# A scan kernel on one core: the chunk tables are read after the weight steps, and two groups of scan inputs begin two and three half slots sooner

## The chip, the cores and the metric

The kernel runs on one core of one Trainium2 chip. The metric is the device time of one execution in microseconds (us). TensorE is called PE, VectorE DVE, ScalarE ACT, GpSimd POOL, and SyncE, which here issues the transfers, SP.

## What is computed

Two transformer blocks run over `x` of shape (2, 1024, 512). The first half of block 0 is a gated delta-rule scan over 1024 positions for each of two batches, with 64 state columns; everything that the change touches belongs to it.

```python
k = _l2norm(x @ Wk.T); v = x @ Wv.T; q = _l2norm(x @ Wq.T)
alpha = exp(8 * sigmoid(x @ Wa_w.T + Wa_b) * log(sigmoid(lam) + 1e-8))
def step(H, inp):                      # one position
    pred = einsum('bk,bkv->bv', q_t, H)
    surprise = sigmoid(sum((v_t - pred) ** 2))
    delta = k_t[:, :, None] * (v_t - einsum('bk,bkv->bv', k_t, H))[:, None, :]
    H = a * H + (1.0 - a) * (surprise * delta)
    return H, einsum('bk,bkv->bv', q_t, H)
...
wq_gu = ternary_quant(w_gate_up); wq_p = ternary_quant(w_proj)   # the weights of the feed-forward part of block 0
```

After the scan come that block's feed-forward part with ternary weights, then block 1 (an attention part with a running sum, and a feed-forward part).

## The kernel before

`head()` does three things at once: it prepares the inputs of the scan, it runs the first half of the scan, and it turns the first layer's weights into ternary ones. `groups()`, which is not touched, does the second half of the scan and all the rest.

**Scan.** A batch's 1024 positions are eight chunks of 128. `head()` does chunks 0 to 3 (`HC = 4`) of both batches. A chunk is solved by five rounds (`R = 5`). In a round each batch b goes through one chain: PE multiplies (`residual`, L659, two matmuls written as four passes), DVE subtracts (`residual`, L929 in the first round, L932 in the others), ACT squares and takes a tanh (`surprise`, L470 and L472), DVE weighs (`weighted`, L943), and PE may multiply again. Behind the fifth round of a chunk a new state is made (PE `states` L668, DVE L954, then PE L659 on the new state), and in the first round of the next chunk PE also makes two outputs (`outputs`, L677 and L678).

**Half slots.** The order of each engine's queue is written out by hand by the number h of a half slot. Half slot h = 2 * (n * R + r) + b belongs to round r of chunk n of batch b, so that 40 half slots, 0 to 39, make up the scan, ten for a chunk. Half slots from -28 to -1 come before it. On DVE the order in a pair is: `residual` of batch 0, inputs(h), late(h), `residual` of batch 1, `weighted` of batch 0, inputs(h + 1), late(h + 1), `weighted` of batch 1. On PE it is `residual`, means(h), inputs(h), sections(h), and behind these `states` and `outputs` where there are any.

**Inputs of the scan.** Four groups u = 0 to 3 of 512 positions are prepared in stages i, and `BEGIN` says in which half slot a group reaches stage 10:

```python
    BEGIN = (-26, -18, 6, 16)
...
    def stages(h):
        return [(u, h - BEGIN[u] + 10) for u in range(NG)]
```

Groups 0 and 1 feed the four chunks of this scan; groups 2 and 3 feed the chunks that `groups()` does later. The stages are: 0 to 4 statistics (DVE L721 to L729), 6 to 9 normalization (DVE L737), 10 to 13 feature-major turns (PE L552, ACT L378), 14 to 17 projections (PE L568, four matmuls each), 18 to 25 DVE and ACT work on them with the cumulated sum in 20 (PE L582, L586), and then for each of the group's four chunks a transposition (PE L596 to L599 in stages 25, 27, 29, 31, copied out by ACT L418 and L419) and a product (PE L605 in stages 26, 28, 30, 32). DVE reads the product's bank `in_t1`, multiplies by a mask and writes the chunk's table `LT`:

```python
        def masked(u, j):
            dve.wait_ge(l_full, u * NJ + j + 1)
            ...
            nc.vector.tensor_tensor(at_chunk(scan, "LT", ORDER[u] * NJ + j), pl[:, 0:3 * P].rearrange("p (k t) -> p k t", t=P),
                                    mask[:], ALU.mult).then_inc(l_out, 1)
```

The next product into that bank waits for `l_out`, and so do some turns of the features that use the same bank.

**Weights.** 112 ternary steps (`ternary`, L829 to L842, one DVE instruction of 128x512 or 128x1024 each) are dealt out evenly over half slots -18 to 39 by `late(h)`, mostly two to a half slot; `means(h)` is their matmul L614 on PE. `late(h)` also finishes one section of the modulation in half slot 7 (L104, which signals `mod_out`); the first projection of group 2 waits for that signal.

Of the kernel before, what the change touches and what calls it, by code (L numbers as in the profile page):

```python
# [124 lines left out]
def head(nc, dram, keep, scan, sems, whole, ctx):  # L125
# [96 lines left out]


    HALVES = 2 * HC * R
    BEGIN = (-26, -18, 6, 16)
    FROM, TERNARY_FROM, SECTIONS_FROM = -28, -18, -7
    STEPS = WSTEPS * PAIRS

    def stages(h):

        return [(u, h - BEGIN[u] + 10) for u in range(NG)]

# [5 lines left out]
    def ternary_step(n):  # L238

        if n == 0:  # L240
            return 0, 0
        q, i = divmod(n - 1, WSTEPS)
        if q == PAIRS - 1:
            return q, i + 1
        return (q + 1, 0) if i == 3 else (q, i + 1 if i < 3 else i)
# [3 lines left out]
    def late_section(h):  # L249

        n, stage = divmod(h - SECTIONS_FROM, KD + 1)
        return (n + 2, stage) if 0 <= n < EARLY_SECTIONS - 2 else (None, None)
# [106 lines left out]
    def _(act):  # L359
# [73 lines left out]
        def log_decays():  # L433
            act.wait_ge(lam_sig, 3)
            nc.scalar.activation(lam[:], lam[:], ACT.Ln).then_inc(act_steps, 1)
            act.wait_ge(consts, 6)
            nc.scalar.activation(junk[0][:, 0, 0:1], ones[:, 0:1], ACT.Exp)
# [48 lines left out]
        for h in range(FROM, 0):  # L486
            if h == BEGIN[0] + KD:
                log_decays()
# [226 lines left out]
    def _(dve):  # L715
        c = Count(dve, dve_steps)

        def norm_stats(u, j):
            if j == 0:
                dve.wait_ge(x_in[u % 2], 16 * (u // 2) + 16)  # L720
            c.did(nc.vector.bn_stats(stats[:, j], x[:, u % 2, j]))  # L721
# [28 lines left out]
        def values(u):  # L750
            dve.wait_ge(proj, u + 1)
            nc.vector.tensor_copy(chunk(scan["v"], u), pp[:, :, 2 * NS:3 * NS]).then_inc(v_out, 1)
# [68 lines left out]
        def ternary(q, i):  # L821


            if (q, i) != (0, 0):
                dve.wait_ge(w_steps, number[q, i] - 1)
            wt, scale = keep["wt"][:, 2 * q:2 * q + 2], wscale[:, q % 2]
            if i < 2:
                dve.wait_ge(mean_full, 2 * q + i + 1)
                ins = nc.vector.tensor_scalar(scale[:, i], pm[0], 1e-8, None, ALU.max, ALU.max,  # L829
                                              accum_out=wsmax[:, 2 * q + i:2 * q + i + 1])  # L830
            elif i == 2:
                ins = nc.vector.tensor_tensor(whash[:], scale, wabs[:, q % 2], ALU.is_lt)
            elif i == 3:
                dve.wait_ge(w_cast, 3 * q + 2)
                ins = nc.vector.tensor_tensor(whash[:], whash[:], wsgn[:, q % 2], ALU.mult)
            elif i == 4:
                ins = nc.vector.tensor_tensor(whash[:], whash[:], scale, ALU.mult)
            elif i == 5:
                dve.wait_ge(w_cast, 3 * q + 3)
                ins = nc.vector.tensor_tensor(whash[:], whash[:], wt, ALU.subtract)  # L840
            else:
                ins = nc.vector.tensor_tensor(wt, wt, whash[:], ALU.add)  # L842
            ins.then_inc(w_steps, 1)
# [46 lines left out]
        def inputs(h):  # L890
            for u, i in stages(h):
                if u and 0 <= i < NJ:
                    norm_stats(u, i)
                elif u and i == 4:
                    norm_sums(u)
                elif u and 6 <= i < 6 + NJ:
                    norm_rows(u, i - 6)
                elif i == 18:
                    gate_in(u)
                    values(u)  # L900
                elif i == 19:
                    lengths(u)
                    log_alphas(u)
                elif i == 20:
                    keys(u, 0)
                    keys(u, 1)
                elif i == 21:
                    before(u)
                    betas(u, 0)
                elif i == 22:  # L910
                    betas(u, 1)
                    if u:
                        growths(u).then_inc(ready, 1)
                    else:
                        c.did(growths(u))
                elif i in (23, 24):
                    tilted(u, 2 * (i - 23))
                    tilted(u, 2 * (i - 23) + 1)
                elif i == 25:
                    spans(u, 0)  # L920
                    spans(u, 1)
                elif i in (26, 28, 30, 32):
                    masked(u, (i - 26) // 2)

        def residual(n, r, b):
# [37 lines left out]
        def late(h):  # L963
            for i in share(h, STEPS):
                ternary(*ternary_step(i))
            if late_section(h)[1] == KD:
                section(late_section(h)[0])

        for h in range(FROM, 0):
            if h == BEGIN[0] + 8:  # L970
                log_decays()
            inputs(h)
            late(h)
        for n in range(HC):
            for r in range(R):
                h = 2 * (n * R + r)
# [1492 lines left out]
def build(nc, dram):  # L2469
    with ExitStack() as whole:  # L2470
# [46 lines left out]
        with ExitStack() as ctx:  # L2517
            head(nc, dram, keep, scan, sems, whole, ctx)
# [58 lines left out]
```

## Time and profile before

| what | us |
|---|---|
| median of 3 runs | 1183.12 (1183.0 to 1185.53) |
| the profiled execution | 1185.58 |
| its span, first to last instruction | 1184.0 |
| up to the scan's first DVE instruction (L929 at 77.30) | 77.3 |
| the 40 half slots of the scan, 77.30 to 200.07 | 122.8 |
| everything behind it | 983.9 |

PE is busy for 1077.5 us of the span, DVE for 869.1, ACT for 525.2 and POOL for 171.3. These are averages over stages that differ: the scan in `head()` is a chain that passes between PE, ACT and DVE for two batches in turn, with the other work laid in between. What an edit is worth there is read from which wait ends last in a half slot.

### The profile page before, as it was taken

The numbers are of one execution on the slowest core, as the hardware profiler recorded it, in microseconds if no ns is written. First come the engines' busy times: TensorE is split into PE (matmuls) and PEld (weight loads), VectorE is DVE, ScalarE is ACT, GpSimd is POOL, SyncE is SP. The second block draws the span as 40 slices with busy tenths as digits, with TensorE's granted clock in tenths as the row PEclk, the third lists the DMA queues.
The fourth block names the chain that finished last, engine by engine and source line by source line (L and its number), as shares of the span: only waits on it lengthen the run. The fifth ranks groups of instructions, "written<-read, shape, count | busy, mean of one in ns | idle before, by whom it ended". The sixth has DMA issues, their size and how long they took to land. (4 is left out here: it accounts for less than half of the span.)

```text
span 1184.0 us, 12999 instructions
## 1 busy us (share of the span) xinstructions
PE 1077.5 (91%) x4360; PEld 522.0 (44%) x4360; DVE 869.1 (73%) x1602; ACT 525.2 (44%) x1103; POOL 171.3 (14%) x143
## 2 busy tenths in 40 slices
PE   6788778799979999888998999999998999999997
PEld 2435545444534444334443454444444444444443
DVE  3887776756756778797687899577887677785654
ACT  3655654445525385244263364164444263531421
POOL 3100000211202221030121131122102000100100
PEclk9888765699998999899998999999999999999999
DMA  8511111532400333222130003012010011010000
GB/s 272 180 54 36 54 36 27 187 107 72 126 0 19 118 92 104 69 79 89 56 95 18 27 27 98 16 40 101 27 63 10 1 60 30 18 72 0 1 36 35
DMA packets 47618, 75.53 MB, mean 64 GB/s; under 512 B 8416, under 2 KB 16096, under 8 KB 47424
## 3 DMA queue, kind: packets, MB, share of 16 engines
q1 hardware_dynamic: 47264, 74.62, 19.9%
q0 software_dynamic: 288, 0.09, 0.2%
q8 instruction: 35, 0.57, 0.2%
q14 instruction: 31, 0.25, 0.1%
HBM read 66.16 MB, written 8.54 MB: 63 GB/s over the span
## 5 line engine op out<-in xcount | busy, mean ns | idle before, releaser
L1517 PE MATMUL g_g<-h,wt 128*128 128x512 f16 x1728 | 401.2, 381 | 5.8 <-DVE hid L1824 3.1
L1517 PEld LDWEIGHTS g_g<-h,wt 128*128 128x128 bf16 (+1 forms) x1728 | 168.4, 98 | 223.8 <-issue 35.5
L1531 PE MATMUL g_d<-wt,parts 128*128 128x512 bf16 (+1 forms) x864 | 208.5, 384 | 4.5 <-DVE tmp L1654 2.7
L2144 ACT ACTIVATE parts<-hid 128x512 f16<-128x512 f32 x108 | 68.0, 629 | 303.3 <-DVE hid L1824 303.2
L1439 PE MATMUL g_o<-shared 128*128 128x512 f32 x384 | 183.3, 621 | 14.4 <-DVE tmp L1613 6.4
L1817 DVE SCALAR_TENSOR_TENSOR hid<-th,g_g 128x512 f32<-128x512 f32 x108 | 73.6, 681 | 135.8 <-ACT th L2137 135.7
L1531 PEld LDWEIGHTS g_d<-wt,parts 128*128 128x128 f16 x864 | 84.1, 99 | 114.5 <-issue 16.6
L2258 POOL TENSOR_TENSOR acc<-acc,sqh 128x512 f32<-128x512 f32 x52 | 79.6, 1532 | 297.1 <-ACT sqh L2150 297.1
L1439 PEld LDWEIGHTS g_o<-shared 128*128 128x128 f32 x384 | 75.0, 199 | 98.4 <-issue 72.5
L1829 DVE TENSOR_TENSOR parts<-hid,parts 128x512 f16<-128x512 f32 x108 | 89.6, 830 | 26.0 <-ACT parts L2144 25.9
L2238 POOL TENSOR_TENSOR g_rstd<-g_var,g_power 128x4 f32<-128x4 f32 x20 | 24.2, 1210 | 328.9 <-DVE g_var L1557 328.9
L1824 DVE SCALAR_TENSOR_TENSOR hid<-hid,fac,g_g 128x512 f32<-128x512 f32 x64 | 46.9, 732 | 23.6 <-PE g_g L1517 22.7
L2137 ACT ACTIVATE th<-g_g 128x512 f32<-128x512 f32 x64 | 37.6, 588 | 51.7 <-PE g_g L1517 51.5
L1448 PE MATMUL g_o<-shared 128*128 128x512 f32 x128 | 57.8, 594 | 2.7 <-DVE shared L1901 2.7
L2137 ACT ACTIVATE th<-g_g,sgate 128x512 f32<-128x512 f32 x44 | 30.1, 684 | 62.2 <-PE g_g L1517 62.2
L1892 DVE RECIPROCAL shared<-shared 128x256 f32<-128x256 f32 x32 | 55.8, 1743 | 0.0
L2246 POOL TENSOR_TENSOR h<-hf,h 128x512 f16<-128x512 f32 x32 | 41.2, 1293 | 85.1 <-ACT hf L2037 79.2
L2157 ACT ACTIVATE shared<-g_o 128x512 f32<-128x512 f32 x32 | 19.0, 593 | 62.4 <-PE g_o L1439 62.3
L1824 DVE SCALAR_TENSOR_TENSOR hid<-hid,sgu,g_g 128x512 f32<-128x512 f32 x44 | 32.0, 728 | 16.4 <-PE g_g L1517 16.0
L1569 DVE TENSOR_TENSOR x<-x,tmp 128x512 f32<-128x512 f32 x60 | 39.9, 688 | 1.0
L2150 ACT ACTIVATE sqh<-hid 128x512 f32<-128x512 f32 x64 | 39.3, 614 | 0.4 <-PE g_o L1428 0.3
L1847 DVE SCALAR_TENSOR_TENSOR shared<-shared,mix 128x512 f32<-128x512 f32 x48 | 36.8, 809 | 2.4 <-ACT shared L2065 2.3
(329 smaller groups left out, 1511.5 us busy)
## 6 DMA issues: line engine op xcount, KB each, us to landing
shared<-in_w SPq DMA_DIRECT2D x48, 256.0 KB, 2.7
x<-in_codes SPq DMA_DIRECT2D x32, 264.0 KB, 3.1
w_raw<-in_wt SPq DMA_DIRECT2D x16, 512.0 KB, 3.5
x<-in_wmod SPq DMA_DIRECT2D x7, 1024.0 KB, 5.2
wmod<-in_wmod SPq DMA_DIRECT2D x5, 1024.0 KB, 11.5
codes_f<-x SPq DMA_DIRECT2D x32, 132.0 KB, 1.7
gates<-in_x SPq DMA_DIRECT2D x4, 1024.0 KB, 8.2
shared<-in_wt SPq DMA_DIRECT2D x8, 512.0 KB, 4.7
```

The costliest lines, as they stand in the source:

```text
L1439: mm = nc.tensor.matmul(dst[:], w1[:, n % 4, k], xmix[:, w, k], start=(k == 0), stop=(k == KD - 1))
L1448: mm = nc.tensor.matmul(dst[:], rw[:, k, j * P:(j + 1) * P], wo[:, k, :], start=(k == 0), stop=(k == KD - 1))
L1517: mm = nc.tensor.matmul(pg[i][:], wide[:, k, o:o + P], h16[f % 2][:, s, k], start=(s == 0 and k == 0), stop=(s == 1 and k == KD - 1))
L1531: mm = nc.tensor.matmul(pd[j][:], parts16[:, t % 3, s, j * P:(j + 1) * P], wd[:, m, :], start=(m == 0 and s == 0), stop=(done and s == 1))
L1817: nc.vector.scalar_tensor_tensor(hid[:, t % 2], th[:], 1.0, pg[0][:], ALU.add, ALU.mult).then_inc(gate_free, 1)
L1824: nc.vector.scalar_tensor_tensor(hid[:, t % 2], hid[:, t % 2], const, pg[1][:], ALU.mult, ALU.mult).then_inc(up_free, 1)
L1829: nc.vector.tensor_tensor(parts16[:, t % 3, 1], hid[:, t % 2], parts16[:, t % 3, 0], ALU.subtract).then_inc(lo_ready, 1)
L1892: c.did(nc.vector.reciprocal(part, part))
L2137: nc.scalar.activation(th[:], pg[0][:], ACT.Tanh, scale=scale).then_inc(th_ready, 1)
L2144: nc.scalar.activation(parts16[:, t % 3, 0], hid[:, t % 2], ACT.Copy).then_inc(hi_ready, 1)
L2246: nc.gpsimd.tensor_tensor(h16[f % 2][:, 1, k], hf[:, k % 2], h16[f % 2][:, 0, k], ALU.subtract).then_inc(hl_ready, 1)
L2258: nc.gpsimd.tensor_tensor(acc[:], acc[:], sqh[:, m % 2], ALU.add).then_inc(acc_ready, 1)
```

## The change

The read of the product's bank is taken out of the stages and put in a function of its own, `tables(h)`, which DVE runs behind the ternary steps of the half slot. `BEGIN` of group 2 goes from 6 to 4, and that of group 3 from 16 to 13, on all engines. No instruction is added or removed; PE's, ACT's, DVE's and POOL's work is the same, in another order.

```diff
-    BEGIN = (-26, -18, 6, 16)
+    BEGIN = (-26, -18, 4, 13)
     FROM, TERNARY_FROM, SECTIONS_FROM = -28, -18, -7
@@
                 elif i == 25:
                     spans(u, 0)
                     spans(u, 1)
-                elif i in (26, 28, 30, 32):
+
+        def tables(h):
+            for u, i in stages(h):
+                if i in (26, 28, 30, 32):
                     masked(u, (i - 26) // 2)
@@
         def late(h):
             for i in share(h, STEPS):
                 ternary(*ternary_step(i))
+            tables(h)
             if late_section(h)[1] == KD:
                 section(late_section(h)[0])
```

Four lines are added ahead of them, so L929, L932, L943, L954 and L961 of before are L932, L935, L946, L957 and L964 in the changed kernel.

The first place is DVE's queue in the last chunk of the scan, half slots 34 to 36. In the kernel before:

```order
L932 TENSOR_TENSOR shared<-shared,sc 128x128
L812 TENSOR_TENSOR shared<-in_t,mask 128x384
L832 TENSOR_TENSOR whash<-wscale,wabs 128x1024
L835 TENSOR_TENSOR whash<-whash,wsgn 128x1024
L932 TENSOR_TENSOR shared<-shared,sc 128x128
L943 SCALAR_TENSOR_TENSOR shared<-shared,sur 128x64
L829 TENSOR_SCALAR wscale,wsmax<-mean_ps 128x512
L837 TENSOR_TENSOR whash<-whash,wscale 128x1024
L943 SCALAR_TENSOR_TENSOR shared<-shared,sur 128x64
L932 TENSOR_TENSOR shared<-shared,sc 128x128
L812 TENSOR_TENSOR shared<-in_t,mask 128x384
L840 TENSOR_TENSOR whash<-whash,wt 128x1024
```

The same half slots, 34 to 36, in the changed kernel:

```order
L935 TENSOR_TENSOR shared<-shared,sc 128x128
L832 TENSOR_TENSOR whash<-wscale,wabs 128x1024
L835 TENSOR_TENSOR whash<-whash,wsgn 128x1024
L935 TENSOR_TENSOR shared<-shared,sc 128x128
L946 SCALAR_TENSOR_TENSOR shared<-shared,sur 128x64
L829 TENSOR_SCALAR wscale,wsmax<-mean_ps 128x512
L837 TENSOR_TENSOR whash<-whash,wscale 128x1024
L812 TENSOR_TENSOR shared<-in_t,mask 128x384
L946 SCALAR_TENSOR_TENSOR shared<-shared,sur 128x64
L935 TENSOR_TENSOR shared<-shared,sc 128x128
L840 TENSOR_TENSOR whash<-whash,wt 128x1024
L842 TENSOR_TENSOR wt<-wt,whash 128x1024
```

Group 3's table reads (L812) stood directly behind `residual` of batch 0 in half slots 32, 34, 36 and 38. They now stand behind the ternary steps in half slots 29, 31, 33 and 35, ahead of `weighted` of batch 1, and half slots 36 to 39 have none.

The second place is PE's queue at the end of the second chunk and the start of the third (half slots 18 to 20; `residual` is L659, a projection L568 x4, a feature turn L552 x4, a chunk's transposition L596 to L599, its product L605). Before:

```order
L659 MATMUL sc<-shared,LT 128x64 x2
L552 MATMUL in_t<-ident,gates 128x128 x4
L659 MATMUL sc<-shared,LT 128x64 x2
L614 MATMUL mean_ps<-wabs,groupmean 128x512
L552 MATMUL in_t<-ident,gates 128x128 x4
L668 MATMUL sc<-shared 64x64
L659 MATMUL sc<-shared 128x64 x2
L614 MATMUL mean_ps<-wabs,groupmean 128x512
L568 MATMUL in_proj<-w,ln_hT 128x256 x4
L668 MATMUL sc<-shared 64x64
```

In the changed kernel:

```order
L614 MATMUL mean_ps<-wabs,groupmean 128x512
L596 MATMUL in_t<-ident,kq_sq 64x128
L597 MATMUL in_t<-ident,kq_sq 64x128
L598 MATMUL in_t<-ident,qy_tilde 64x128
L599 MATMUL in_t<-ident,b_tilde 64x128
L568 MATMUL in_proj<-w,ln_hT 128x256 x4
L668 MATMUL sc<-shared 64x64
L659 MATMUL sc<-shared 128x64 x2
L614 MATMUL mean_ps<-wabs,groupmean 128x512
L605 MATMUL in_t<-shared,bT 128x384
L568 MATMUL in_proj<-w,ln_hT 128x256 x4
L668 MATMUL sc<-shared 64x64
```

Group 3's projections have moved from half slots 20 to 23 to half slots 17 to 20, and group 2's first transposition and first product, from 21 and 22, now stand in 19 and 20 ahead of the two matmuls L668 that make the new states.

The third place is DVE's queue ahead of the scan, where group 0's third table read and group 1's stage 22 stand (half slot -6). Before:

```order
L829 TENSOR_SCALAR wscale,wsmax<-mean_ps 128x512
L812 TENSOR_TENSOR LT<-in_t,mask 128x384
L785 TENSOR_TENSOR wt<-wt 128x256
L880 TENSOR_TENSOR g<-eh 64x3
L885 TENSOR_SCALAR gh<-g 64x3
L832 TENSOR_TENSOR whash<-wscale,wabs 128x1024
L835 TENSOR_TENSOR whash<-whash,wsgn 128x1024
L793 TENSOR_TENSOR wt<-shared,wt 128x4x64 x2
```

In the changed kernel:

```order
L829 TENSOR_SCALAR wscale,wsmax<-mean_ps 128x512
L785 TENSOR_TENSOR wt<-wt 128x256
L880 TENSOR_TENSOR g<-eh 64x3
L885 TENSOR_SCALAR gh<-g 64x3
L721 BN_STATS ln_stats<-gates 128x6
L832 TENSOR_TENSOR whash<-wscale,wabs 128x1024
L835 TENSOR_TENSOR whash<-whash,wsgn 128x1024
L812 TENSOR_TENSOR LT<-in_t,mask 128x384
L793 TENSOR_TENSOR wt<-shared,wt 128x4x64 x2
```

The table read has moved behind six instructions of its half slot, one of which (L721, group 2's first statistics) comes from half slot -4.

## Rows read from the trace of the kernel before

**Rows 1.** Windows by stage: length, busy time and count by engine, PE clock, DMA.

```profile
77.30:105.38 28.08, 22.48 (x99) 11.67 (x97) 24.39 (x72) 18.17 (x50) 1.39 (x1) 0.83 0.12 39
105.38:136.16 30.78, 24.08 (x116) 19.46 (x117) 24.11 (x74) 19.30 (x61) 3.23 (x2) 0.78 0.14 52
136.16:171.34 35.18, 28.56 (x124) 20.16 (x123) 25.41 (x71) 19.13 (x66) 1.85 (x1) 0.74 0.16 46
171.34:200.07 28.73, 25.46 (x80) 16.40 (x79) 20.77 (x54) 14.34 (x56) 0.00 (x0) 0.50 0.08 19
```

**Rows 2.** DVE's waits in the scan (77.3 to 200.07): total us, times, longest.

```profile
DVE shared L932 <- PE sc L659: 8.0, 7, 2.5
DVE shared L812 <- PE in_t L605: 7.2, 8, 1.3
DVE shared L929 <- PE sc L659: 5.8, 6, 1.2
DVE shared L954 <- PE sc L668: 3.7, 2, 1.9
DVE LT L812 <- PE in_t L605: 1.6, 3, 1.1
```

**Rows 3.** Timeline of DVE, 190 to 195.3 us: start, duration, what, [idle before].

```profile
190.15 0.28 DVE L932 TENSOR_TENSOR shared<-shared,sc 128x128 f32<-128x128 f32 x1
...
191.49 0.56 DVE L812 TENSOR_TENSOR shared<-in_t,mask 128x384 f32<-128x384 f32 x1 [1.06 <-PE in_t L605]
...
193.29 0.28 DVE L932 TENSOR_TENSOR shared<-shared,sc 128x128 f32<-128x128 f32 x1
...
195.22 0.28 DVE L932 TENSOR_TENSOR shared<-shared,sc 128x128 f32<-128x128 f32 x1
```

**Rows 4.** Timeline of PE over the same round, 188.7 to 193.9 us.

```profile
188.76 1.11 PE L659 MATMUL sc<-shared,LT 128*128 128x64 f32 x4
189.81 1.65 PE L605 MATMUL in_t<-shared,wt 64*128 64x384 f32 x2
191.38 1.11 PE L659 MATMUL sc<-shared,LT 128*128 128x64 f32 x4
192.29 0.63 PE L614 MATMUL mean_ps<-wabs,groupmean 128*128 128x512 bf16 x1
192.71 0.42 PE L596 MATMUL in_t<-ident,wt 128*64 128x128 f32 x1
...
193.35 0.42 PE L599 MATMUL in_t<-ident,wt 128*64 128x128 f32 x1
...
193.82 1.11 PE L659 MATMUL sc<-shared,LT 128*128 128x64 f32 x4
```

**Rows 5.** Timeline of PE and DVE: projections, a product, and a new state at a chunk's start.

```profile
105.27 3.78 PE L568 MATMUL in_proj<-w,ln_hT 128*128 128x256 f32 x8
...
136.46 3.62 PE L568 MATMUL in_proj<-w,ln_hT 128*128 128x256 f32 x8
...
140.41 0.28 DVE L954 SCALAR_TENSOR_TENSOR shared<-sc,gh,shared 64x64 f32<-64x64 f32 x1 [1.82 <-PE sc L668]
...
145.69 0.91 PE L605 MATMUL in_t<-shared,bT 64*128 64x384 f32 x2
...
149.19 1.89 PE L568 MATMUL in_proj<-w,ln_hT 128*128 128x256 f32 x8
```

**Rows 6.** Timeline at half slots 7 to 9: the last early section and what follows.

```profile
98.82 0.16 DVE L104 TENSOR_SCALAR modv<-in_proj 128x8 f32<-128x8 f32 x1
99.44 1.12 PE L659 MATMUL sc<-shared,LT 128*128 128x64 f32 x4 [1.08 <-DVE shared L943]
101.42 0.28 DVE L932 TENSOR_TENSOR shared<-shared,sc 128x128 f32<-128x128 f32 x1
```

**Rows 7.** Timeline of DVE ahead of the scan: the longest table wait there.

```profile
62.78 0.56 DVE L812 TENSOR_TENSOR LT<-in_t,mask 128x384 f32<-128x384 f32 x1 [1.55 <-PE in_t L605]
```

**Rows 8.** Window of the long stretch in which PE's granted clock is 0.50.

```profile
157.20:222.00 64.80, 52.42 (x164) 33.82 (x163) 46.52 (x132) 28.74 (x104) 3.16 (x4) 0.50 0.33 105
```

## The prediction

> **What bounds the kernel now.** I read the windows by stage first. The change touches only `head()`: the 77.3 us ahead of the scan, and the scan's four chunks of 28.08, 30.78, 35.18 and 28.73 us, 122.8 in all [rows 1]. What comes later has the same queues, so it should move as a block with the end of the scan. In the scan no engine is full: DVE is busy for 24.39, 24.11, 25.41 and 20.77 us of the four chunks, 94.7 of 122.8. The list of DVE's waits says where the other 28 are: 8.8 us in 11 waits for a table's product (7.2 + 1.6), 13.8 for the residual matmuls (8.0 + 5.8) and 3.7 for the new states [rows 2]. Only the 8.8 is what the moved table read waits for.
>
> Next I read the last chunk, where the pattern is clean. Batch 0's residual is subtracted at 190.15, DVE waits 1.06 us for the product, reads it at 191.49, does two ternary steps and takes batch 1's residual at 193.29; the other half slot, without a table, lasts from 193.29 to 195.22 [rows 3]. A round is 5.06 us. PE in such a round: residual of batch 0 from 188.76, product from 189.81, residual of batch 1 from 191.38, mean from 192.29, transposition from 192.71, next residual at 193.82 [rows 4]. The last of the transposition's four passes, which follow each other by 0.21, starts at 193.35, so PE could have gone on at 193.56. It is full for 4.80 of 5.06 us. So the visible DVE wait of 1.06 is worth only 0.26 per round as long as the round holds a product and a transposition.
>
> **The parts of the change, each costed.**
>
> *Ahead of the scan: -1.0 us.* The longest table wait there is 1.55 us [rows 7]. Behind it DVE has work that needs nothing of the product: two ternary steps, 1.3 us together (193.29 less 191.49 and the 0.5 that a read keeps DVE [rows 3]), and group 1's stage 22. Taken in front they cover all of it, at most -1.55. Against it, group 2's sums (some 0.5 us of small DVE instructions) are now done before half slot 0. If PE or ACT is late next, nothing is left: 0 is the other bound.
>
> *First chunk, 28.08 us: +1.5.* Group 2's first two projections come to half slots 8 and 9. The first waits for the section signal at 98.82, while PE would start batch 1's residual at 99.44 and DVE take it at 101.42 [rows 6]. A row L568 x8 is one projection, four matmuls in two passes each: 3.6 us of PE at the lower clock, 1.8 at the upper (3.62 and 1.89 [rows 5], whose last pass overlaps what follows by 0.1). At the lower clock PE is at the residual at 98.9 + 3.6 = 102.5 and DVE gets it at about 103.3, 1.9 us late; at the upper clock it is there at 101.4 and costs nothing. To this come 0.65 us more of DVE's stage work in this chunk, and some 0.6 us of table waits go. Bounds 0 and +3; I take +1.5, since the residual at 99.44 takes 1.12 us [rows 6], the lower clock's time (1.11 at 188.76 [rows 4], where the clock is 0.50 [rows 8]).
>
> *Second chunk, 30.78 us: +0.5.* Group 3's first three projections come to half slots 17 to 19 and leave 21 to 23. These half slots were 2.2 to 2.5 us long, filled by DVE; a projection of 1.8 beside a residual of 0.5 fits, one of 3.6 does not and costs 2.4. In both runs of four projections the first one is long (105.27 and 136.46); the other six are short like the last (149.19 [rows 5]). With one long one, half slot 17 costs +2.4. Half slot 10 then has group 2's third projection in place of its first and saves 1.8. Bounds -1.5 and +5 (all three long); I take +0.5.
>
> *Third chunk, 35.18 us: -4.5.* Here PE holds 9.8 us of DVE's time (35.18 less 25.41). Three projections leave half slots 21 to 23, where DVE waited for residuals behind them, and the table waits are covered by 1.3 us of ternary steps. What has to stay is the latency of the states, about 1 us for each first residual (L929: 5.8 in 6 times [rows 2]). New is that in half slot 20 a product stands with the last projection ahead of L668, for which DVE already waits 1.82 us [rows 5]. At the upper clock mean, projection and product are 0.2 + 1.8 + 0.9 behind the residual, and the state is ready some 3.1 us after it instead of 4.25 (136.16 to 140.41). So DVE's busy time of 25.4, 0.5 more of stage work, and about 3.5 of waits: 29.4, a gain of 5.8. At the lower clock half slot 20 is 1.8 us worse than now, the cumulated sum in 23 is 1 us longer, and the gain is 2. I take 4.5, nearer to the first, because the run of projections has begun three half slots earlier.
>
> *Last chunk, 28.73 us: -3.5.* The four rounds from 180.1 on last 20.2 us. Two of them keep a product and a transposition and stay PE's: 4.80 each. The other two, half slots 36 to 39, are bare: 1.93 us (193.29 to 195.22) and 1.5 (3.13 of the half slot from 195.22, less a wait of 1.05 and the read's 0.5), 3.45 a round. That makes 16.5, a gain of 3.7. In half slots 30 and 31, a product of 1.57 takes the place of a transposition of 0.85 ahead of the outputs, with DVE idle behind it: +0.7, less what DVE's two moved instructions of stage 24 (0.67) free in half slot 30. Bounds -2.8 and -4.2. The read in an odd half slot stands ahead of batch 1's `weighted`; by PE's order (residual, mean, product: 0.9 + 0.4 + 1.6) it is ready 2.0 us after that residual is taken, when two ternary steps and `weighted` (1.8) are nearly through. It costs nothing there while PE is full.
>
> **Sum:** -1.0 + 1.5 + 0.5 - 4.5 - 3.5 = -7.0 us. The profiled execution took 1185.58 around a span of 1184.0 and would take 1178.6. It lies 2.5 above the median of the runs, 1183.12, which gives 1176.1. SP's and POOL's queues keep their order: no transfer is moved past another. POOL's two roots per group come as much sooner as their inputs.
>
> **The clock.** From 157.2 to 222.0 the granted clock is 0.50, the 1.2 GHz level, although PE is busy for 52.4 of these 64.8 us [rows 8] and full for 4.80 of 5.06 in a round [rows 4]. The Trainium skill says otherwise: its page TensorE: Matmul & The Clock Gate (Part 1: The HAM clock gate) has sustained activity release the throttle and idleness bring it back, and by it the rounds from 180 on would be at 2.4 GHz. The trace does not agree there; by that rule the two full rounds would shrink from 4.80 to DVE's own 3.9 each (3.45 and a read of 0.5), 1.8 us more gained. By the same rule the emptier half slots 12 to 16 of the changed kernel would send the projections behind them to the lower level, which speaks against the change. The sum above rests on the rows, and the two directions are the last two rivals.
>
> **The rivals.**
>
> *A, the forecast* (-3 to -11, about 1176): a chance of 0.60.
>
> *B, the waits only change their name* (0.16). PE holds the rounds, the table waits come back as waits for residuals, and group 3's work in the middle costs what it frees at the end. For it: 4.80 of 5.06 [rows 4]. Against it: the two bare rounds and the three projections that leave the crowded third chunk. It gives 4 x 0.26 = 1 for the waits and about 1 for the rest, -2: 1181.
>
> *C, slower: the projections run at the lower clock* (0.10). Half slots 12 to 16 keep only small PE work and the clock falls ahead of half slot 17. Each further long projection costs 1.8 us on PE. Today two of eight are long; with six of eight that is 7.2, which is the whole gain, and half slot 20 at the lower level adds 1.8 plus 0.8 for the product: +3, 1186. The point from which it decides is four further long ones. For it: with two levels, means of 0.83, 0.78 and 0.74 say that PE is at the lower one for a third to a half of the first three chunks, and for all of the last (0.50 [rows 1]). Against it: each run so far has risen after its first.
>
> *D, more* (0.14): the clock stays at the upper level into the last chunk or nearly all projections find it. The last chunk's full rounds shrink by 1.8 and the others reach their bounds: -12, 1171.
>
> **The numbers.** The likeliest is 1176.1. The low end adds the good bounds, -1.5 + 0 - 1.5 - 5.8 - 4.2 = -13, 1170; the high end the bad ones short of all at once, -0.5 + 3 + 2 - 2 - 2.5 = 0, stretched by 1 for C: 1184. A's own range is 1172 to 1180. A measurement of this kernel tells 0.2% (2.4 us) from no change, that is, below 1180.8 is faster. Of A nearly all, all of D and a third of B are faster: 0.78. The rest of B and the mild end of C are the same: 0.13. Slower: 0.09.
>
> **What would show it.** The scan's first subtraction should come at 76.3 and the second chunk's start later than 105.38 - 1.0 by 1 to 2 us. From the 20th half slot to the 30th it should take some 31 us, and from the 30th to the end 25, with the last two rounds near 3.5 each. Table reads should have almost no wait of their own in the half slots with two ternary steps, except in half slots 20 and 29 to 35. Of the eight projections two or three should have rows of 3.6. The prediction is wrong if the clock's pattern in half slots 8 to 23 puts more than four projections at the lower level, if the waits for L668 in half slots 19 and 20 grow by more than a microsecond each, or if what follows the scan does not move with it.

## The result and the profile after

| what | before | after |
|---|---|---|
| median of 4 runs each, us | 1184.32 (1183.0 to 1186.87) | 1170.39 (1164.84 to 1171.01) |
| ratio, 95% interval | | 0.9878 (0.9857 to 0.9898) |
| the profiled execution and its span | 1185.58, 1184.0 | 1170.35, 1168.8 |

The changed kernel is 13.9 us faster. The forecast was 7.0, so the time, 1170.4, lies at the low edge of the range, twice as far down as predicted. The windows by stage of the changed kernel have the columns of [rows 1]; the fifth row is all that lies behind the scan.

```profile
77.73:104.09 26.36, 22.68 (x113) 12.84 (x115) 24.72 (x72) 18.25 (x50) 1.39 (x1) 1.00 0.13 43
104.09:132.49 28.40, 23.67 (x126) 19.54 (x128) 24.31 (x70) 20.04 (x64) 1.85 (x1) 0.88 0.15 54
132.49:162.85 30.36, 27.22 (x100) 18.00 (x102) 25.55 (x73) 18.92 (x66) 1.85 (x1) 0.60 0.20 53
162.85:188.20 25.35, 22.30 (x74) 15.10 (x74) 19.51 (x50) 13.45 (x53) 0.00 (x0) 0.50 0.09 22
188.20:1168.80 980.60, 916.15 (x3702) 425.62 (x3739) 722.51 (x1193) 415.05 (x804) 150.78 (x109) 0.97 0.18 57
```

The scan's end is taken here at batch 0's last new state (L957; batch 1's follows 1.03 us behind it in both kernels). Before, it stood at 200.21, 0.14 us behind the end in [rows 1]. Counted so, the four chunks are 1.7, 2.4, 4.8 and 3.5 us shorter, and none is longer. DVE is busy for 94.1 us of them, as long as before (94.7), in 12.4 us less. The list of DVE's waits in the scan answers to [rows 2] (us, times, longest):

```profile
DVE shared L935 <- PE sc L659: 7.7, 9, 2.8
DVE shared L932 <- PE sc L659: 6.0, 7, 1.2
DVE shared L957 <- PE sc L668: 1.1, 1, 1.1
DVE shared L812 <- PE in_t L605: 0.5, 2, 0.3
```

The waits for a table's product fell from 8.8 us to 0.5. The waits for residuals (L935 and L932, before L932 and L929) stayed at 13.7, so the table waits did not come back under that name. In DVE's timeline the round that answers to [rows 3] looks like this (half slots 34 to 36, and the bare round behind them):

```profile
176.72 0.29 DVE L935 TENSOR_TENSOR shared<-shared,sc 128x128 f32<-128x128 f32 x1 [0.30 <-PE sc L659]
...
178.32 0.29 DVE L935 TENSOR_TENSOR shared<-shared,sc 128x128 f32<-128x128 f32 x1
...
180.32 0.56 DVE L812 TENSOR_TENSOR shared<-in_t,mask 128x384 f32<-128x384 f32 x1
...
181.36 0.29 DVE L935 TENSOR_TENSOR shared<-shared,sc 128x128 f32<-128x128 f32 x1 [0.29 <-PE sc L659]
...
182.90 0.28 DVE L935 TENSOR_TENSOR shared<-shared,sc 128x128 f32<-128x128 f32 x1
...
184.82 0.28 DVE L935 TENSOR_TENSOR shared<-shared,sc 128x128 f32<-128x128 f32 x1
```

A full round takes 181.36 less 176.72, 4.64 us (before 5.06, forecast 4.80), a bare one 184.82 less 181.36, 3.46 (forecast 3.45). The read at 180.32 waits for nothing. PE's rows of this round follow each other without a gap from one residual of batch 0 to the next, 175.57 to 180.21, which is 4.64 as well:

```profile
175.57 1.11 PE L659 MATMUL sc<-shared,LT 128*128 128x64 f32 x4
...
178.64 1.65 PE L605 MATMUL in_t<-shared,wt 64*128 64x384 f32 x2
```

So PE does fill such a round, but with 4.64 us: the 4.80 of [rows 4] had 0.16 us of slack in it. Last, the projections on PE, which answer to [rows 5]:

```profile
98.11 1.99 PE L568 MATMUL in_proj<-w,ln_hT 128*128 128x256 f32 x8 [0.90 <-DVE modv L104]
...
103.98 1.99 PE L568 MATMUL in_proj<-w,ln_hT 128*128 128x256 f32 x8
...
107.21 1.99 PE L568 MATMUL in_proj<-w,ln_hT 128*128 128x256 f32 x8
...
128.42 1.89 PE L568 MATMUL in_proj<-w,ln_hT 128*128 128x256 f32 x8
...
133.55 1.99 PE L568 MATMUL in_proj<-w,ln_hT 128*128 128x256 f32 x8
```

None of the eight takes 3.6 us. I had expected two or three long ones, and priced one in the first chunk and one in the second. A single trace can show luck, so both kernels were profiled again.

### The profile page after: what moved, and what is told of

The parts are those of the page before. It is cut to its first block and busy times, and to the rows that moved or that the text cites. A ratio compares the mean times of both kernels' runs of the same rounds, so it can differ in the third digit from the quotient of the medians.

```text
span 1168.8 us, 12951 instructions
## 1 busy us (share of the span) xinstructions
PE 1069.0 (91%) x4312; PEld 518.6 (44%) x4360; DVE 868.8 (74%) x1602; ACT 524.7 (45%) x1103; POOL 171.6 (15%) x143
## 3 DMA queue, kind: packets, MB, share of 16 engines
q1 hardware_dynamic: 47264, 74.62, 20.2%
## 5 line engine op out<-in xcount | busy, mean ns | idle before, releaser
L1535 PE MATMUL g_d<-wt,parts 128*128 128x512 bf16 (+1 forms) x831 | 201.0, 383 | 7.2 <-DVE tmp L1658 2.7
L1443 PE MATMUL g_o<-shared 128*128 128x512 f32 x384 | 183.3, 621 | 14.4 <-DVE tmp L1617 6.4
L2242 POOL TENSOR_TENSOR g_rstd<-g_var,g_power 128x4 f32<-128x4 f32 x20 | 24.2, 1211 | 328.8 <-DVE g_var L1561 328.8
L2141 ACT ACTIVATE th<-g_g,sgate 128x512 f32<-128x512 f32 x44 | 30.1, 685 | 62.3 <-PE g_g L1521 62.2
```

What stands on the lines that cost most here:

```text
L1443: mm = nc.tensor.matmul(dst[:], w1[:, n % 4, k], xmix[:, w, k], start=(k == 0), stop=(k == KD - 1))
L1535: mm = nc.tensor.matmul(pd[j][:], parts16[:, t % 3, s, j * P:(j + 1) * P], wd[:, m, :], start=(m == 0 and s == 0), stop=(done and s == 1))
L2141: nc.scalar.activation(th[:], pg[0][:], ACT.Tanh, scale=scale).then_inc(th_ready, 1)
```

## The experiments

Times are medians of the runs, ratios are to the kernel before, run beside each, with the 95% interval. "Before" was timed 4 to 19 times in each comparison, with medians from 1183.4 to 1185.2 us. The trace of a kernel is of one of these runs, and not always of one near the median: with group 3 at 15 and with group 2 left at 6 it is of the slowest (1174.8 and 1181.8 us), with the tables alone of the fastest.

**Which half of the change does it?** One theory says that the gain above the forecast is the granted clock's and the two edits are worth about what the sum gave; the other that both edits free DVE by themselves.

```diff
 # after, tables behind the ternary steps, groups as before
-    BEGIN = (-26, -18, 4, 13)
+    BEGIN = (-26, -18, 6, 16)
```

> The kernel before with the table reads moved behind the ternary steps, and BEGIN left at 6 and 16. Theory 1 (the gain is above all PE's clock during the projections, which the shifted groups change): this half alone brings little, 1 to 3 us, because PE fills the rounds of the last chunk (4.80 of 5.06 us), and the first projections of half slots 10 and 20 stay long (3.6 us). Rival (the waits for the tables' product were the cost, the clock followed by chance): 7 us or more, most of the 8.8 us of waits.

```diff
 # before, tables in front, groups as after
-    BEGIN = (-26, -18, 6, 16)
+    BEGIN = (-26, -18, 4, 13)
```

> The kernel before with BEGIN at 4 and 13, and the table reads left at the front of their half slot. Theory 1: nearly the whole gain, 8 to 11 us, with all eight projections short (1.9 us); group 3's reads in half slots 29 to 35 now stand behind batch 1's residual and ahead of the ternary steps and cost a wait each again. Rival: 3 to 5 us, the two bare rounds at the end alone.

The tables alone: 1178.37 us, ratio 0.9949 (0.993 to 0.9968), that is -6.0. The groups alone: 1178.08, 0.9956 (0.9932 to 0.9979), -5.2. Both are faster, and neither carries the gain by itself; of the two theories the first gave the tables 1 to 3 us and the groups 8 to 11, the second 7 or more and 3 to 5, and the two measured values fit neither pair. Their sum is -11.2 and the whole change gives -14.4 (0.0122 of 1184). The 3 us between are no more than the intervals of the three ratios allow (each 2.3 to 2.8 us to either side), so a part that the edits have only together isn't shown by the times. The windows and DVE's waits of the kernel with the tables alone (the traced execution took 1170.96 us; a second trace is in the table further below):

```profile
74.71:100.35 25.64, 20.69 (x98) 10.96 (x98) 24.10 (x72) 18.29 (x50) 1.39 (x1) 0.89 0.13 43
100.35:131.18 30.83, 24.00 (x114) 19.61 (x117) 24.10 (x75) 19.30 (x61) 3.23 (x2) 0.78 0.15 51
131.18:164.18 33.00, 27.23 (x122) 19.64 (x123) 25.05 (x72) 19.19 (x66) 1.85 (x1) 0.76 0.17 49
164.18:191.20 27.02, 24.42 (x80) 16.66 (x80) 21.47 (x55) 14.68 (x56) 0.00 (x0) 0.50 0.08 21
```

```profile
DVE shared L935 <- PE sc L659: 9.7, 9, 2.5
DVE shared L932 <- PE sc L659: 5.9, 6, 1.2
DVE shared L957 <- PE sc L668: 3.8, 2, 1.9
```

No table read waits any more, 8.8 us before; residual waits rise from 13.8 to 15.6 (20.1 in the second trace, whose first chunk is 4.8 us longer). The third chunk is 2.2 and the last 1.8 us shorter than before, both counted to the same end, and the second is unchanged. The granted clock in the third and the last is nearly as before (0.76 and 0.50). So "the waits only change their name" is false in these two chunks, and the 0.26 us a round that I allowed for a covered wait was too little: half slots 32 to 39 took 18.58 us here and 20.42 before, 0.46 a round.

The kernel with the groups alone, windows and then waits:

```profile
78.24:108.00 29.76, 25.41 (x113) 14.95 (x114) 24.99 (x72) 18.14 (x50) 1.39 (x1) 0.89 0.15 43
108.00:136.40 28.40, 23.71 (x126) 19.61 (x128) 24.31 (x71) 20.04 (x64) 1.86 (x1) 0.88 0.14 49
136.40:170.42 34.02, 27.55 (x100) 17.66 (x102) 25.57 (x72) 18.85 (x66) 1.86 (x1) 0.59 0.16 47
170.42:197.37 26.95, 22.88 (x74) 15.06 (x74) 19.17 (x50) 13.39 (x53) 0.00 (x0) 0.50 0.10 21
```

```profile
DVE shared L812 <- PE in_t L605: 10.6, 8, 1.7
...
DVE LT L812 <- PE in_t L605: 0.7, 2, 0.4
```

Its second chunk is that of the changed kernel (28.40); its third and last are 3.7 and 1.6 longer, with PE's clock and busy time nearly the same (0.59 against 0.60, 27.55 against 27.22). What differs is the place of the read. Group 3's reads now fall into odd half slots in front of the ternary steps, as in DVE's timeline in half slot 33, and table waits grow to 11.3 us:

```profile
183.25 0.56 DVE L812 TENSOR_TENSOR shared<-in_t,mask 128x384 f32<-128x384 f32 x1 [1.52 <-PE in_t L605]
```

Half slots 33 and 35 last 4.00 and 3.76 us there, 3.05 in the changed kernel. That is the 1.6 us of the last chunk, and no more than the later place of the read gives with the groups at their old places (1.8), so nothing there appears only together. In the third chunk the later place gives 2.2 us at the old places and 3.7 at the new ones, but against the changed kernel's four traces (28.64 to 31.51) the 3.7 is anything from 2.5 to 5.4. This kernel also has the long projection that I had priced:

```profile
99.49 3.78 PE L568 MATMUL in_proj<-w,ln_hT 128*128 128x256 f32 x8 [1.03 <-DVE modv L104]
```

Half slot 8 lasts 4.30 us with it and 2.16 in every trace of the changed kernel. The price that I gave it, +1.9, was right (it is 2.1); that it would come in the changed kernel was wrong. PE's queue is the same in both kernels, so the order on PE alone doesn't decide whether this row is long.

**How far must the groups move?**

```diff
 # after, group 3 one half slot sooner than before; then: group 2 not moved
-    BEGIN = (-26, -18, 4, 13)
+    BEGIN = (-26, -18, 4, 15)
...
+    BEGIN = (-26, -18, 6, 13)
```

> The changed kernel with group 3 beginning at 15 instead of 13, so that group 2's shift stands nearly alone. Theory 1: group 2's four projections in half slots 8 to 11 are short as in the changed kernel, so the first chunk and the second keep what they gained up to half slot 16 (about 4 us in all); the last chunk has one bare round instead of two and the crowding of half slots 19 to 22 is back in part. 5 to 8 us faster than before. Rival (group 3's place makes the gain): 2 to 4.

> The changed kernel with group 2 back at 6 and group 3 at 13. Group 2's first projection stands in half slot 10 behind light half slots 7 to 9 again. Theory 1: its row is long (3.6 us) or not by what PE did before, and the time is 2 to 4 us above the changed kernel's; 8 to 11 faster than before. Rival (group 2's shift is worth nothing): level with the changed kernel.

Group 3 at 15: 1171.09 us, 0.9891 (0.9875 to 0.9906). Group 2 left at 6: 1173.86, 0.9915 (0.9885 to 0.9945). The first can't be told from the change as made, though its chunks are others: 30.58 for the second (a projection of 3.62 at its end), 30.89 and 26.77 for the last two; both theories had expected less of it (5 to 8 us, 2 to 4) than the 12.9 that it gives. The tables with group 3 moved give 10 of the 14 us, where the tables alone gave 6; group 2's two half slots add some 4 (0.9915 less 0.9878). That last part is the least sure: the two intervals overlap a little, and the seven times without it lie in two clusters, 1168.5 to 1173.9 and 1179.4 to 1181.8.

```diff
 # after, group 3 one half slot sooner still
-    BEGIN = (-26, -18, 4, 13)
+    BEGIN = (-26, -18, 4, 12)
```

> The changed kernel with group 3 at 12 instead of 13, one half slot sooner still, and so with its table reads back in even half slots 28 to 34. Theory (bare half slots at the end are cheap, 1.5 to 1.9 us): 1 us less in the last chunk; the second chunk gets the fourth projection (half slot 19, ahead of a new state) and half slot 20 loses it: 1 to 2 us faster than the changed kernel. Rival: the crowding in half slots 16 to 19 takes it back, same within 1 us.

1170.91 us, 0.9893 (0.986 to 0.9926): no difference to 13 or 15 that can be measured.

**Does more work on PE hold the clock up?** The kernel before, where each mean matmul of weight pairs 5 to 10 (from 73.6 us, just ahead of the scan, to the end of its second chunk) is made three times, with the same result:

```diff
             # PE, mean(q, i)
+            for _ in range(2 if 5 <= q <= 10 else 0):
+                nc.tensor.matmul(pm[0], groupmean[:], wabs[:, q % 2, i], start=True, stop=True)
```

> The kernel before, in which PE does each mean matmul (L614, 128x512 bf16, 0.2 us at the upper clock) three times in a row in about half slots 0 to 20, with the same result; DVE, ACT and the order are untouched. PE gets 0.4 us more work per mean, in half slots that DVE fills. Theory (the clock during the projections made the gain of the first two chunks): the projections of half slots 10 and 20 become short, and the first two chunks together lose 2 to 4 us, although PE has more to do. Rival (the clock does not matter there, or does not follow PE's load): the chunks stay at 28.1 and 30.8 or get longer by the added work.

1182.43 us, 1.0004 (0.9971 to 1.0037): no gain. The windows of the traced execution:

```profile
77.50:108.50 31.00, 26.38 (x111) 12.18 (x111) 24.60 (x71) 18.20 (x51) 1.39 (x1) 0.83 0.10 35
108.50:138.57 30.07, 25.36 (x126) 20.21 (x127) 24.21 (x74) 19.30 (x61) 3.23 (x2) 0.81 0.15 53
138.57:176.33 37.76, 31.14 (x124) 21.95 (x123) 25.39 (x71) 19.13 (x66) 1.85 (x1) 0.68 0.15 42
```

The first projection of group 2, long in [rows 5], became short, and half slot 10 went from 5.15 to 3.22 us. But half slot 4 took 5.70 us and the third chunk 37.76, so in this execution what was won in one place was lost in two others. It took 1193.0 us, one of four at 1192.6 to 1195.6 with a mean granted clock of 0.930 to 0.933; the other eight took 1179.6 to 1183.7 with 0.941 to 0.947, and none of these was traced. So the median of 1182.43 stands for the eight, and what their chunks look like isn't known.

**How much do traces of one kernel differ?** Both kernels and the tables alone, unchanged:

> The kernel before once more, for a second trace. If the long projections at half slots 10 and 20 come from the order of the work, they are long here too. If they come from where the clock's changes happen to fall in an execution, the first chunk, the second chunk or both differ by a microsecond or more, with other rows long.

> The changed kernel once more, for a second trace. If all eight projections are short again, the clock in the first two chunks follows from the new order; if one or more take 3.6 us, it was the fall of the clock's changes in that execution. The stretch behind the scan, 3 us shorter in the first trace than in that of before, shows by its clock whether it differs again.

> The kernel before, a third trace. Two traces have the stretch ahead of the scan at 77.3 and 79.3 us, the first chunk at 28.1 and 29.9, and what follows the scan at 983.8 both times. Theory (the stretch behind the scan depends only on where the clock's changes fall against the scan's end, not on the change): this trace may have another length there, between 978 and 986.5, with the end of the long low stretch 21 to 25 us behind the scan's end. Rival (the kernel before always loses 4 to 5 us there): 983.8 again.

> The changed kernel, a third trace. Second chunk 28.4 and last chunk 25.4 us again, as both times. The stretch behind the scan anywhere between 978 and 986.5 by the theory of the clock's fall, 978 to 981 by the rival.

> Only the table reads moved, a second trace; the first was of the fastest of seven runs. The last two chunks should be at 33.0 and 27.0 again (the part of the 6 us that is the order's), while the stretch ahead of the scan and the first chunk, 74.7 and 25.6 in the first trace, should be longer by 1 to 4 us together.

The single times were 1188.08 and 1180.32 us for before, 1166.11 and 1168.6 for after, 1178.31 for the tables alone. By stage, from the windows (us; "ahead" is up to the scan's first subtraction, the end of the scan batch 0's last new state; the fourth trace of the changed kernel is from a run told further below):

| kernel | ahead | chunks 1 to 4 | behind |
|---|---|---|---|
| before | 77.30 | 28.08, 30.78, 35.18, 28.87 | 983.79 |
| again | 79.31 | 29.94, 29.76, 34.85, 28.85 | 983.79 |
| third | 77.95 | 26.68, 29.90, 34.62, 28.86 | 980.79 |
| after | 77.73 | 26.36, 28.40, 30.36, 25.35 | 980.60 |
| again | 74.97 | 28.84, 28.40, 28.64, 25.36 | 978.39 |
| third | 77.14 | 26.36, 28.40, 31.51, 25.35 | 978.24 |
| fourth | 75.68 | 26.38, 28.41, 31.47, 25.36 | 978.30 |
| tables alone | 74.71 | 25.64, 30.83, 33.00, 27.02 | 978.20 |
| again | 74.64 | 30.47, 30.78, 32.86, 27.05 | 981.00 |

The second and the last chunk repeat within 0.01 us after the change. The first has two values there, 26.4 and 28.8, by half slot 4, which lasts 2.6 or 5.1 us. Before, it has three: 26.68, 28.08 and 29.94, with 2.6, 3.6 and 4.9 us in half slot 4. Without that half slot the first chunk takes 24.1 to 25.1 us before and 23.8 in all four traces after. In the second trace of the changed kernel DVE waits there, where it waited for nothing in the first:

```profile
90.75 0.29 DVE L935 TENSOR_TENSOR shared<-shared,sc 128x128 f32<-128x128 f32 x1 [2.40 <-PE sc L659]
```

In that trace a pair of section matmuls at 88.31 takes 1.82 us, and the same pair in the first trace, at 88.69, 1.02: PE was at the lower level there (0.50 from 83.1 to 89.9). The third chunk varies too, in part by whether group 3's last projection is long. PE in the third trace of the changed kernel:

```profile
132.11 0.91 PE L605 MATMUL in_t<-shared,bT 64*128 64x384 f32 x2
132.95 3.46 PE L568 MATMUL in_proj<-w,ln_hT 128*128 128x256 f32 x8
136.34 0.48 PE L668 MATMUL sc<-shared 128*64 128x64 f32 x2
```

Half slot 20 is 6.0 us with it, as in the fourth trace, and 4.39 without. The rest lies in half slots 21 to 25: with the same half slot 20 they are 1.9 us shorter in the second trace (28.64) than in the first (30.36), and the long low stretch of the clock begins at 144.6 there, 12.4 us into the chunk, and at 138.6 in the first, 6.1 into it. So seven or eight of eight projections are short after the change; the one of half slot 8 and those of half slots 17 to 19 in all four traces.

**Can the clock be brought up in the last chunk?** On the changed kernel each mean matmul from weight pair 10 on (from 122.0 us; that is half slot 17, where the expectations say 19) is made four times:

```diff
             # after, PE, mean(q, i)
+            for _ in range(3 if q >= 10 else 0):
+                nc.tensor.matmul(pm[0], groupmean[:], wabs[:, q % 2, i], start=True, stop=True)
```

> The changed kernel, in which PE does each mean matmul four times in a row from half slot 19 on, with the same result. PE gets up to 1.3 us more work per mean at the lower clock. Theory (more PE work brings the upper level back in the scan's last 45 us, as the Trainium skill's page on the clock gate would have it): the long low stretch is broken, half slot 31 falls from 5.6 to below 5, and the last chunk is not longer than 25.4. Rival (the low stretch does not answer to this work): the clock stays at 0.50, the rounds with a product and a transposition grow by the added work, and the kernel is 5 us or more slower than the changed one.

> The changed kernel with each mean matmul done four times from half slot 19 on, timed again beside the changed kernel itself. Theory (the clock in the last stretch is worth what the one trace showed): last chunk 23.5 instead of 25.4 us and 1.5 to 3 us faster than the changed kernel. Rival (it was where the clock's changes fell): last chunk between 23.5 and 26, time level with the changed kernel within 1 us.

> The changed kernel once more, timed, as the base for the other two. Ratio 0.986 to 0.990 as at first; second chunk 28.4 and last chunk 25.4 us; first chunk 26.4 where half slot 4 takes 2.6 us, 28.8 where it takes 5.1.

```diff
             # as above, and three times for pairs 3 to 6 (ahead of the scan and in half slots 1, 2 and 4)
+            for _ in range(3 if q >= 10 else 2 if 3 <= q <= 6 else 0):
```

> As e13, and in addition each mean matmul done three times from about half slot -11 to 8. Theory (PE work keeps the upper level through half slot 4): half slot 4 takes 2.6 to 3.2 us, first chunk 26.4 to 27, and the time is 0.5 to 1.5 us below that of e13. Rival (the added work only delays PE there, which waits for sections and copies): half slot 4 at 5 us or more, first chunk 28 to 30, slower than e13.

| kernel | us, runs | ratio |
|---|---|---|
| more means late | 1169.35 (4) | 0.9887 (0.9834 to 0.9939) |
| the same again | 1166.16 (6) | 0.9859 (0.9819 to 0.9899) |
| more means early and late | 1168.99 (6) | 0.9885 (0.9853 to 0.9918) |
| the changed kernel, timed again | 1168.85 (6) | 0.9879 (0.9848 to 0.9910) |

The last chunk of the first trace of this kernel, and of the second:

```profile
162.16:185.69 23.53, 19.57 (x90) 11.82 (x89) 19.01 (x50) 13.39 (x53) 0.00 (x0) 0.79 0.09 24
```

```profile
162.30:192.52 30.22, 26.89 (x89) 16.00 (x90) 19.44 (x51) 13.45 (x53) 0.00 (x0) 0.56 0.08 18
```

In the first, PE comes back to the upper level for a part of the chunk (0.79), and the chunk is 1.8 us shorter than 25.36; the last kernel of the table did the same (23.91). In the second, one queue and one program (1177.4 us, the second slowest of its six), the clock stays low (0.56), and the chunk is 4.9 us longer. The ratios are the same as that of the changed kernel within their intervals. So no version was found that is faster than the change as made. For the early means nothing could be told: half slot 4 was short (2.60), but so it is in three of the four traces without them.

## Why the prediction was right in its direction and half in its size

Means over the traces of the table, three before and four after, against the terms of the sum:

| term | forecast | measured |
|---|---|---|
| ahead of the scan | -1.0 | 78.19 to 76.38: -1.8 |
| first chunk | +1.5 | 28.23 to 26.98: -1.25 |
| second chunk | +0.5 | 30.15 to 28.40: -1.75 |
| third chunk | -4.5 | 34.88 to 30.50: -4.4 |
| last chunk | -3.5 | 28.86 to 25.36: -3.5 |
| behind the scan | 0 | see below |

*The step that failed* is the pair "First chunk, 28.08 us: +1.5" and "Second chunk, 30.78 us: +0.5". Each rests on one projection at the lower clock, in half slots 8 and 17, and neither came: in all four traces of the changed kernel both are short. Together the two terms were to cost +2.0 and gave -3.0: 5.0 of the 5.7 us by which the head differs from the sum. I read from two runs of four projections that "the first one is long", and took that for a property of being first. The runs show that it isn't: it is short in half slots 8 and 17 here. Nor is it the place alone: the groups alone have a long one in half slot 8 with the same PE queue, and first ones are long in half slots 16 (group 3 at 12) and 19 (group 3 at 15), too, here the one in 16:

```profile
122.71 3.56 PE L568 MATMUL in_proj<-w,ln_hT 128*128 128x256 f32 x8
```

In half slots 10 and 20 they are long in all three traces of before and both of the tables alone. So a row is long where a low stretch of the clock falls on it, and where that happens I can't derive from the order. The rest of the working of these two terms held, but for one reading: of half slots 17 to 19, "2.2 to 2.5 us long" before, the last took 4.03, since the new state is made there. Half slot 10 was to save 1.8 and went from 5.15, 4.61 and 4.74 us to 3.22 each time; half slot 17, priced at +2.4, lasts 2.60 against 2.45. With both long projections at 0 the same sum gives -1.0 + 0 - 1.8 - 4.5 - 3.5 = -10.8. Of the 1.9 us that this still lacks, 1.25 are the first chunk's. There 0.5 is half slot 4 (3.7 us in the mean of the three traces before, 3.2 of the four after), which each kernel has short in some traces and long in others, so that part is luck of the traces taken; 0.8 is in the other nine half slots, where the table waits went and DVE's busy time rose by 0.3 us (24.39 to 24.72), not by the 0.65 that I had set against them.

*The third chunk* was sized right in the mean, where the single traces are 3.4 to 6.2 us below the mean of before. Half slot 20 with its product ahead of L668 costs 4.4 or 6.0 us by its projection, against 4.9 to 5.3 before, and the wait for L668 in it is 1.12 us in two traces and 2.7 in the other two, against the 1.82 of [rows 5]; I had taken the lower clock there to cost 1.8 more than before, and it costs 0.7 to 1.1.

*The last chunk* was nearly right in its parts: half slots 32 to 39 take 16.1 us (forecast 16.5), with a floor of 4.64 in place of 4.80 for a full round, and took 20.42 before, not 20.2 (they begin at 179.79, not at 180.1); half slots 30 and 31 are 0.8 longer (forecast 0.7, less what two moved instructions free). The two misses in its gain, +0.6 and -0.5, cancel.

*Ahead of the scan* nothing more than the sign is known. Queues that are the same there took 74.6 and 74.7 us (tables alone) and 78.1 (group 2 left at 6). In the first trace after, the reads there wait for nothing, as forecast.

*Behind the scan* I had forecast nothing. The queues are the same, and still that stretch took 978.0 to 986.3 us over 17 traces of all kernels. From near the two ends of the scale, rows of windows: group 2 left at 6, and the fourth trace of the changed kernel.

```profile
194.07:1180.20 986.13, 921.95 (x3702) 429.89 (x3739) 722.36 (x1193) 415.44 (x804) 150.56 (x109) 0.97 0.19 57
```

```profile
187.30:1165.60 978.30, 914.59 (x3702) 426.22 (x3739) 721.76 (x1193) 414.99 (x804) 150.97 (x109) 0.97 0.19 58
```

DVE and ACT are as busy; PE is busy for 7.4 us more. Summed from the trace's records of the clock, it is at 0.50 for 68.0 us behind the scan in the first and for 53.3 in the second, 14.7 more, and half of that is the 7.4. Over all traces the time at 0.50 behind the scan is 53.0 to 56.0 us in the twelve that took 978.0 to 981.0, and 62.2 to 68.1 in the five that took 983.3 to 986.3. It goes with a second number, how long the low stretch at the scan's end reaches behind it. [Rows 8] end at 222.0, the scan at 200.21: 21.8 us, and 983.79. The second trace of before has 21.9 and 983.79 as well. In the changed kernel the stretch is

```profile
138.60:210.30 71.70, 60.74 (x193) 40.11 (x196) 55.62 (x155) 36.05 (x130) 4.16 (x5) 0.50 0.30 96
```

and ends 22.1 behind the scan (188.20), with 980.60. With 22.3 to 22.5 it took 980.8 to 981.0 (third trace of before, tables alone again), with 22.9 to 23.3 it took 978.0 to 978.6 (six traces), with 24.0 to 24.2 979.1 to 979.3 (three), with 24.3 986.1 and 986.3, with 24.6 983.3. Kernels with unlike heads agree to about 0.2 us where this number agrees, but a step of 0.1, from 24.2 to 24.3, goes with 7 us. So the stretch moves by up to 8 us with where the clock's changes fall on its matmuls. Which edit brings which value can't be planned from a trace of before.

*The sum of it:* the head gives -12.7 by the traces, and the timed ratios -14.4 (0.9878 and 0.9879). Behind the scan the mean of the traces fell by 3.9, which is more than the 1.7 us between. How much of that comes with the change, and how much is which traces happened to be taken, isn't settled.

*Of the rivals,* B, which gave the covered waits 1 us, fell by the tables alone (-6.0), C by the short projections. D named the time, 1171, and half its cause: nearly all projections find the upper level, but the last chunk stays at 0.50 throughout, as in [rows 8]. A held in its mechanism, with two of its terms of the wrong sign. That the clock makes the gain, the theory I tested first, fell as well: the last two chunks give 7.9 of the 12.7 us, and the clock there is no higher after (0.60 and 0.50) than in [rows 1] (0.74 and 0.50). In the second chunk it does count: half slot 10 is 1.4 to 1.9 us shorter, with a projection of 1.99 us in it in place of one of 3.4 to 3.8. Else what the clock did was not to take what I had charged to it.

What stays open: why the clock is low at half slot 4 in some executions of one and the same program, and what makes it low at a group's first projection in half slots 10, 16, 19 and 20, but in 8 and 17 of the changed kernel not.

## What to carry to other kernels

In queues that are written out by hand, put an instruction that reads another engine's result behind as much independent work of its own half slot as there is: with the tables alone 8.8 us of visible waits became none and gave 6.0 us by the timed ratio, give or take 2.3, of which 4.0 are seen in the last two chunks, although PE seemed full for 4.80 of 5.06 us of a round. Price a clock-bound step (here a projection of 1.9 or 3.6 us) at both of its durations and give each a chance; a pattern of two in one trace ("the first one is long") says little of other places. More traces of before show which long rows repeat there, not which will be long once the order is changed. Where executions of one program differ by 0.5%, take three or four traces before a term under 3 us is put down to an edit.

## What the runs showed of the hardware that was not expected

- A long stretch of small matmuls stayed at the lower clock. In the changed kernel the granted clock is 0.50 for 71.7 us in which PE is busy for 60.7. The added bf16 matmuls of 128x512 broke that stretch in two of three traces of kernels with them (last chunk 23.53 and 23.91 us against 25.36) and not in the third (30.22). The Trainium skill (TensorE: Matmul & The Clock Gate, Part 1: The HAM clock gate) has activity release the throttle; these traces agree only in part, since the same queue did and did not.
- The identical queues behind the scan, 980 us long, differ by 8 us in 17 traces, with 53 to 68 us of them at the lower clock. That is more than half of the gain measured here, and may be why six runs of one kernel spread over 10 us (1164.02 to 1174.13 for the changed one). These six have only one trace, but each has its mean granted clock on record, and it goes the same way: 0.950 for the fastest, 0.943 for the two at 1167.2, 0.940 at 1170.5 and 0.938 for the two at 1174.1. In which stage the slower ones lose their time isn't shown.
